# Reordering the state-space stage of a graph network: other PSUM banks for turned slices, products between the logits, interleaved silus

## The reference, cut to what matters

```
fx = x @ W_fx.T + b_fx ; xm = x @ W_x.T + b_x           # 8 heads of 64
sw = softmax((xm @ W_slice.T + b_slice) / temp)         # node -> 64 slices, per head
st = einsum(fx, sw) / (sw.sum(nodes) + 1e-5)            # 64 slice states of 512 per graph
z, xBC, dt = split(st @ in_w.T)                         # the input projection
dt = softplus(dt + dt_bias)                             # both directions
x, B, C = silu(conv3(xBC) + conv_b)
h_t = h_{t-1} * exp(dt A) + dt B x ; y = C h_t          # a scan over the 64 slices, both ways
y = shifted(y_fw) + shifted(y_bw) + x * (x @ fcD_w.T + D)
yg = y * silu(z) ; yg = yg * rsqrt(mean(yg^2)) * norm_w
out = einsum(yg @ out_w.T, sw) @ out_w2.T + out_b       # back from slices to nodes
x = x + out
```

## Time and profile before

| | us |
|---|---|
| time, median of 3 runs | 4348.56 (4342.05 to 4350.47) |
| the profiled execution's own time | 4347.33 |
| its span, first to last instruction | 4345.6 |
| the stage's 13 steady turns, 473.2 to 1671.8 | 1198.6 |
| TensorE busy over the span | 3361.2 (77%) |

### The profile page before, as it was taken

The page is one execution under the profiler, slowest core; times in us unless marked ns, Lnnn a source line. Parts: engine busy times, 40 slices in busy tenths (PEclk is TensorE's granted clock), DMA queues, the critical chain, the costliest instruction groups (busy, mean ns, idle before and its releaser), DMA issues. The chain is left out here.

```text
span 4345.6 us, 58773 instructions
## 1 busy us (share of the span) xinstructions
PE 3361.2 (77%) x22329; PEld 2135.3 (49%) x22329; DVE 2712.3 (62%) x4371; ACT 1291.7 (30%) x2418; POOL 125.4 (3%) x163
## 2 busy tenths in 40 slices
PE   6257999998998998426627997667777797996998
PEld 5134545445454444215514664544444466774665
DVE  4636776777777777499483334488887443884333
ACT  2113333333333333000214443211111341443444
POOL 0000000000000000000000000012222000000000
PEclk6568898999999999655558998688888896887999
DMA  2111111112111112100102331000000210000322
GB/s 34 42 54 40 45 33 45 33 33 52 33 33 45 33 33 49 39 0 0 33 0 70 73 72 13 1 1 0 0 0 4 57 46 10 2 2 21 81 71 66
DMA packets 139573, 141.55 MB, mean 33 GB/s; under 512 B 63764, under 2 KB 121520, under 8 KB 136904
## 3 DMA queue, kind: packets, MB, share of 16 engines
q1 hardware_dynamic: 139376, 138.68, 13.1%
HBM read 130.64 MB, written 8.01 MB: 32 GB/s over the span
## 5 line engine op out<-in xcount | busy, mean ns | idle before, releaser
L733 DVE TENSOR_TENSOR f_hg<-f_hs,f_gb 128x640 f32<-128x640 f32 x320 | 263.8, 825 | 506.5 <-ACT f_hs L715 448.0
L2046 PE MATMUL hy_ps<-hy_uT,hy_win 128*128 128x512 f32 x1152 | 498.7, 593 | 0.0
L715 ACT ACTIVATE f_hs<-f_ph,f_b1t 128x320 f32<-128x320 f32 x640 | 335.0, 527 | 405.0 <-PE f_ph L683 400.9
L683 PE MATMUL f_ph<-XNP,f_w 128*128 (+1 forms) x1280 | 403.3, 439 | 12.8 <-PEq L573 8.6
L698 PE MATMUL f_po<-f_hg,f_w 128*128 128x320 f32 x1280 | 404.4, 439 | 10.5 <-DVE f_hg L733 10.5
L2046 PEld LDWEIGHTS hy_ps<-hy_uT,hy_win 128*128 128x128 f32 x1152 | 217.6, 190 | 281.4 <-issue 281.4
L683 PEld LDWEIGHTS f_ph<-XNP,f_w 128*128 128x128 f32 x1280 | 246.9, 193 | 117.3 <-issue 18.3
L698 PEld LDWEIGHTS f_po<-f_hg,f_w 128*128 128x128 f32 x1280 | 240.1, 191 | 127.3 <-issue 20.9
L1564 PE MATMUL er_g<-er_TP,er_OT 128*128 128x320 bf16 x768 | 148.7, 338 | 125.8 <-ACT er_OT L1533 125.8
L2107 PE MATMUL hy_ps<-hy_wo,hy_yg 128*128 128x512 f32 x512 | 226.8, 602 | 10.8 <-DVE hy_yg L2358 10.8
L1583 PE MATMUL er_c<-XNG 128*128 128x400 f32 x544 | 211.6, 519 | 9.1 <-POOL XNG L1519 9.1
(11 more groups left out here) (489 smaller groups left out, 5988.6 us busy)
## 6 DMA issues: line engine op xcount, KB each, us to landing
f_gb<-gate_rows SPq DMA_DIRECT2D x32, 1280.0 KB, 8.3
XNG<-hy_decays SPq DMA_DIRECT2D x32, 1024.0 KB
hy_rb<-hy_inverse SPq DMA_DIRECT2D x128, 128.0 KB, 3.1
f_gb<-gate_rows SPq DMA_DIRECT2D x16, 640.0 KB, 5.0
hy_xn<-XNP SPq DMA_DIRECT2D x1, 4096.0 KB
hy_XC<-hy_xn SPq DMA_DIRECT2D x16, 256.0 KB, 3.5
XNG<-in_L_ffn_edge_index_dram SPq DMA_DIRECT2D x2, 2048.0 KB
xin<-in_x_dram SPq DMA_DIRECT2D x5, 512.0 KB, 6.7
```

The source lines that it names most:

```text
L683: pe.matmul(psh[e % 2][k][:], w1[:, e, k * 128:(k + 1) * 128], chunk_view(g, c), start=True, stop=True).then_inc(h_ps, 1)
L715: ins = act.activation(hs[:, e % 2, k, :], psh[e % 2][k][:], ACT.Gelu, bias=b1t[:, e * H2 + k:e * H2 + k + 1])
L733: dve.tensor_tensor(hg[:, e % 2], hs[:, e % 2], gb[:, par, e, None, :].broadcast_to([128, H2, CH]), ALU.mult).then_inc(hg_ready, 1)
L2046: mm = pe.matmul(p[:], win[:, t, m * 128:(m + 1) * 128], uT[:, t, :], start=(t == 0), stop=(t == KT - 1))
```

## The change

Four edits, all inside this stage; no computation is added or left out.

- The turned slices 1 and 2 go to banks 4 and 6 in place of 2 and 3. In exchange there are new waits: for `rn` (bank 4 is read by `inverses`) before slice 1, and for a new semaphore `f_out` (bank 6 is read by `out`) before slice 2. The wait for three copies at pair 1's states goes; a wait for one copy stands before slice 3 is turned, and one for two copies before the input projection.
- `logits` is cut in two halves. TensorE's order is now squares, logits of pairs 0 and 1, gains, logits of pairs 2 and 3.
- The silus of the convolved blocks are taken between the silus of z: block 0 after z's 1, blocks 1 and 2 after z's 2, blocks 3 and 4 after z's 3.
- The mean of squares goes to bank 4 in place of 6 and waits for one copy less (`xt_out` 4k + 7 in place of 4k + 8).

```diff
--- before.py
+++ after.py
@@ -1902,12 +1902,13 @@
         oT = uT[:].rearrange("p k n -> p (k n)")[:, 0:KT * CH].rearrange("p (k q j n) -> p k q j n", q=CHP, j=2, n=N)
         s = {n: sem(n) for n in ("xn_st", "xc", "lf_ps", "lg_out", "smx", "sme", "smd", "sn_ps", "rn", "st_ps", "rn_st", "u_out", "sT_ps", "sT_out",
                                  "ip_ps", "ip_out", "cv", "xs", "dtln", "dt_rdy", "da_exp", "da_rdy", "da_ld", "xt_ps", "xt_out",
-                                 "g_ps", "w_rdy", "y_ps", "yg1", "sq", "sq_sum", "r_ps", "rt", "yg2", "ot_ps", "ot_out", "o_ps", "oT_out", "f_ps", "init", "settled")}
+                                 "g_ps", "w_rdy", "y_ps", "yg1", "sq", "sq_sum", "r_ps", "rt", "yg2", "ot_ps", "ot_out", "o_ps", "oT_out", "f_ps", "f_out", "init", "settled")}
         da_st = [sem(f"da_st{i}") for i in range(2)]
         rb_in = [sem(f"rb_in{q}") for q in range(CHP)]
         half = lambda j: slice(SLOT * j, SLOT * (j + 1))
 
-        TURNED = [5, 2, 3, 5]
+        TURNED = [5, 4, 6, 5]
+        CONVOLVED = [[], [0], [1, 2], [3, 4]]
         ORDER = [IPM - 1] + list(range(KT, 2 * KT + 1)) + list(range(KT))
 
         with nc.Block() as spill:
@@ -1987,11 +1988,12 @@
                     pe.wait_ge(sem, value)
                     pe.sem_inc(s["settled"], 1)
 
-            def logits(k):
-
-                pe.wait_ge(s["xc"], 16 * k + 16)
-                wait(pe, s["sT_out"], 4 * k)
-                for q in range(CHP):
+            def logits(k, f):
+
+                if f == 0:
+                    pe.wait_ge(s["xc"], 16 * k + 16)
+                    wait(pe, s["sT_out"], 4 * k)
+                for q in range(2 * f, 2 * f + 2):
                     if q >= 2:
                         pe.wait_ge(s["lg_out"], 4 * k + q - 1)
                     x = XC[:, q * 128:(q + 1) * 128]
@@ -2018,11 +2020,13 @@
                     mm.then_inc(s["sT_ps"], 1)
 
                 for q in range(CHP - 1):
+                    if q == 1:
+                        settle(s["rn"], k + 1)
+                    elif q == 2:
+                        settle(s["f_out"], k + 1)
                     transposed(q)
                 for q in range(CHP):
-                    if q == 1:
-                        settle(s["sT_out"], 4 * k + 3)
-                    elif q >= 2:
+                    if q >= 2:
                         settle(s["u_out"], 4 * k + q - 1)
                     for j in range(2):
                         for h in range(SH_):
@@ -2031,12 +2035,15 @@
                                            sw[rows(j), q, h * 64:(h + 1) * 64], start=True, stop=True)
                     mm.then_inc(s["st_ps"], 1)
                     if q == 1:
+                        settle(s["sT_out"], 4 * k + 1)
                         transposed(CHP - 1)
 
             def input_projection(k):
                 pe.wait_ge(s["u_out"], 4 * k + 4)
                 for i, m in enumerate(ORDER):
-                    if i == 1:
+                    if i == 0:
+                        pe.wait_ge(s["sT_out"], 4 * k + 2)
+                    elif i == 1:
                         pe.wait_ge(s["sT_out"], 4 * k + 4)
                     if i >= 3:
                         pe.wait_ge(s["ip_out"], IPM * k + i - 2)
@@ -2093,8 +2100,8 @@
             def squares(k):
                 pe.wait_ge(s["sq_sum"], k + 1)
                 if there(k + 1):
-                    pe.wait_ge(s["xt_out"], 4 * k + 8)
-                pe.matmul(PS[6][:], g.mean_w[:], sq[:, 0, :], start=True, stop=True).then_inc(s["r_ps"], 1)
+                    pe.wait_ge(s["xt_out"], 4 * k + 7)
+                pe.matmul(PS[4][:], g.mean_w[:], sq[:, 0, :], start=True, stop=True).then_inc(s["r_ps"], 1)
 
             def output_projection(k):
                 pe.wait_ge(s["yg2"], k + 1)
@@ -2137,10 +2144,12 @@
                     steps_down(c + 1)
                 if there(c):
                     squares(c)
+                if there(c + 2):
+                    logits(c + 2, 0)
                 if there(c + 1):
                     gains(c + 1)
                 if there(c + 2):
-                    logits(c + 2)
+                    logits(c + 2, 1)
                 if there(c):
                     output_projection(c)
                     back_to_nodes(c, par)
@@ -2179,6 +2188,8 @@
                     p = PS[4 + i % 3]
                     if m < KT:
                         act.activation(zs[:, par, m, :], p[:], ACT.Silu).then_inc(s["ip_out"], 1)
+                        for b in CONVOLVED[m]:
+                            convolved(k, b)
                     elif m < IPM - 1:
                         if i == 1:
                             wait(act, s["cv"], XB * k)
@@ -2196,13 +2207,13 @@
                         act.wait_ge(s["dt_rdy"], k + 1)
                         act.activation(dA[:], dtv[:], ACT.Exp, scale=negA[:, 0:1]).then_inc(s["da_exp"], 1)
 
-            def convolved(k):
-                for i in range(KT):
-                    act.wait_ge(s["cv"], XB * k + i + 1)
-                    act.activation(xs[:, i, :], xs[:, i, :], ACT.Silu).then_inc(s["xs"], 1)
-                act.wait_ge(s["cv"], XB * k + XB)
-                act.activation(Cs[:], xs[64:128, KT, :], ACT.Silu)
-                act.activation(xs[0:64, KT, :], xs[0:64, KT, :], ACT.Silu).then_inc(s["xs"], 1)
+            def convolved(k, b):
+                act.wait_ge(s["cv"], XB * k + b + 1)
+                if b < KT:
+                    act.activation(xs[:, b, :], xs[:, b, :], ACT.Silu).then_inc(s["xs"], 1)
+                else:
+                    act.activation(Cs[:], xs[64:128, KT, :], ACT.Silu)
+                    act.activation(xs[0:64, KT, :], xs[0:64, KT, :], ACT.Silu).then_inc(s["xs"], 1)
 
             def steps_down(k):
                 for q in range(CHP):
@@ -2220,7 +2231,7 @@
 
             def root(k):
                 act.wait_ge(s["r_ps"], k + 1)
-                act.activation(rr, PS[6][:], ACT.Sqrt, bias=g.eps[:, 0:1], scale=D / DI).then_inc(s["rt"], 1)
+                act.activation(rr, PS[4][:], ACT.Sqrt, bias=g.eps[:, 0:1], scale=D / DI).then_inc(s["rt"], 1)
 
             def out_copy(k, q):
                 act.wait_ge(s["ot_ps"], 4 * k + q + 1)
@@ -2230,7 +2241,6 @@
                 if there(c + 1):
                     slices(c + 1, 1 - par)
                     projected(c + 1, 1 - par)
-                    convolved(c + 1)
                 if there(c):
                     squares(c)
                 if there(c + 1):
@@ -2250,6 +2260,7 @@
             dve.memset(xr[:], 0.0)
             dve.drain()
             dve.nop().then_inc(s["init"], 1)
+            dve.nop().then_inc(s["f_out"], 2)
 
             def softmax(k):
 
@@ -2368,7 +2379,7 @@
             def out(k):
                 dve.wait_ge(s["f_ps"], k + 1)
                 x = chunk_cols(g.XT, k)
-                dve.scalar_tensor_tensor(x, PS[6][:, 0:CH], outb[:, 0:1], x, ALU.add, ALU.add)
+                dve.scalar_tensor_tensor(x, PS[6][:, 0:CH], outb[:, 0:1], x, ALU.add, ALU.add).then_inc(s["f_out"], 1)
 
             def columns(k):
 

```

## The result

| | before | after |
|---|---|---|
| median of 8 runs each, us | 4349.19 (4342.05 to 4353.46) | 4363.92 (4359.22 to 4370.52) |
| ratio, 95% interval | | 1.0036 (1.0025 to 1.0047) |
| the profiled execution | 4347.33 | 4364.72 |
| the stage's 13 steady turns | 1198.6 | 1217.5 |

What follows compares the result with a forecast made beforehand. TensorE and its clock bound the turns: 91.6 clean, -0.5 front, +2.0 at the logits, +0.4 in `steps_down` make 93.5 against 92.2; with end turns 17 us more, 4364. Range 4338 to 4380, the forecast's own 4354 to 4374.

Steps and rivals of the forecast that it cites:

- What sets the end: Stage's turns: nearly all TensorE, so any gain must come from its 8 us idle a turn or its clock.
- Edit 1, a gain of 0.5: Front of the turn: the 2.14 us wait goes, the last load of inverses then limits; 0.5 us a turn gained.
- Edits 3 and 4 in time: `steps_down` starts without its 1.46 us wait, 2.2 idle inside; squares 1.15 earlier, root unmoved; gain 0 from both.
- The wait at the logits: Ahead of the third pair's logits: TensorE idles 3.1 us in place of 1.97, gain 0.
- The clock at the logits: Third pair's logits: clock falls in every turn, 4.0 us at half speed, 2.0 us a turn lost.
- The clock in `steps_down`: Clock falls there in one turn of three, holding root and `yg` by about 1.2 us: 0.4 a turn.
- Two signs that did not come: Signs for after: mean clock of a turn 0.88 to 0.90; 0.50 at the output projection's start in nearly every turn.
- The sum: Per turn: 91.6 - 0.5 + 2.0 + 0.4 = 93.5 against 92.2; 17 us slower in all, 4364.
- it cancels: Rival: clock falls at the logits, only 1.0 us lost, stays in `steps_down`; 92.1 a turn, 4347; chance 0.20.
- The clock stays: Rival: falls as today, front in all turns, middle in six of 13; 91.4 a turn, 4335; chance 0.17.
- each wait goes for good: Rival: the gate and `yg` come earlier too, 4.75 us a turn gained, 66 in all, 4281; chance 0.02.
- both falls in every turn: Rival: clock falls at logits and in `steps_down` every turn (2.3 and 1.2 us); 94.6 a turn, 4380; chance 0.10.

Runs made afterwards that it cites:

- Edit 1: Only turned slices 1 and 2 moved to banks 4 and 6, with their waits, against the kernel before: 4344.86 us, ratio 0.9996.
- edit 3: Only the silus of convolved blocks interleaved with those of z, against the kernel before: 4363.74 us, ratio 1.0044; once more for its profile, 4361.37.
- edit 4: Only the mean of squares moved to bank 4, waiting for one copy less, against the kernel before: 4346.38 us, ratio 1.0003.
- edit 2: Only the logits split in two halves around the gains, against the kernel before: 4361.94 us, ratio 1.0041.
- dense fillers: Changed kernel plus six unread 128x256 products in the wait ahead of the third pair's logits: 4339.75 us, ratio 0.9981 to the kernel before.
- narrow fillers: Changed kernel plus ten unread 128x8 products in the wait ahead of the third pair's logits: 4366.11 us, ratio 1.0039 to the kernel before.

## Why the prediction was right, step by step

**What sets the end.** Right: the sum was to be made of TensorE's clock, not of the three waits. Waits of 4.75 us a turn went, and the turns grew by 1.45.

**Edit 1, a gain of 0.5: the mechanism held.** The dt products start 9.9 us into a turn in the mean of the 13, 10.7 before, with VectorE's last product waiting for its load (above): 0.8 earlier, not 0.5. But they start at half clock, so a part of that is lost again: the restart of the third pair's logits stands 65.61 us into a turn in the mean, 65.95 in the clean turns of before (816.16 - 750.42 = 65.74 in the one of the earlier trace rows), 0.34 earlier.

**Edits 3 and 4 in time.** Right: `steps_down` starts with no wait, 2.26 us are waited ahead of its third pair (2.2 forecast), and where the clock holds the squares come 6.9 us behind VectorE's gate in place of 8.2, so 1.3 sooner (1.15 forecast), while the root stays at 9.5 behind it.

**The wait at the logits.** 3.1 us forecast, 3.37 measured in the turns without a fall in `steps_down`, 2.1 to 2.5 in the others.

**The clock at the logits: right.** In 13 turns of 13. The third and fourth pair's logits take 5.98 us in the mean and took 3.70, so 2.3 in place of 2.0; in the seven turns with no fall before them it is 5.45, 1.75 more. The dense fillers show that this term is the clock's.

**The clock in `steps_down`: its price right by luck, its place wrong, its count too low.** It fell in 6 turns of 13, not in one of three. These six take 94.3 us in the mean and the other seven 93.1, the 1.2 of the forecast. But the price was said to come through the root and `yg`, held up by 1.2. Measured, the logits' restart is only 0.2 later in the six (65.72 us into the turn against 65.52). Counted from VectorE's gate, which comes 0.3 earlier in the six, root, `yg` and restart are held up by 0.46, where the forecast had 1.2. The other 1.0 comes behind the restart: when the clock has fallen in `steps_down` it comes back and falls again later, and that second fall covers nearly all of the restarted logits, 6.6 us against 5.45. The timeline of a turn without the fall, to set beside the 2.08 us from 817.52 above:

```profile
724.06 2.07 PE L2000 MATMUL hy_ps<-hy_wlg,hy_XC 128*128 128x512 f32 x2 [3.37 <-DVE hy_fx L2270]
725.93 1.72 PE L2001 MATMUL hy_ps<-hy_wfx,hy_XC 128*128 128x512 f32 x2
727.48 1.02 PE L2000 MATMUL hy_ps<-hy_wlg,hy_XC 128*128 128x512 f32 x2
```

The clock is back within the second group. The same groups of the turn from 751.7, the first of which stands above:

```profile
819.39 1.91 PE L2001 MATMUL hy_ps<-hy_wfx,hy_XC 128*128 128x512 f32 x2
821.10 1.91 PE L2000 MATMUL hy_ps<-hy_wlg,hy_XC 128*128 128x512 f32 x2
822.80 1.07 PE L2001 MATMUL hy_ps<-hy_wfx,hy_XC 128*128 128x512 f32 x2
```

Here the third is still at half clock.

**Two signs that did not come.** I had named a mean clock of a turn of 0.88 to 0.90, and 0.50 at the start of the output projection. The turns read 0.91 to 0.94, and the clock is back ahead of the output projection in all 13. The second did not follow from my own numbers: with 4.0 us at half clock the logits themselves take 5.7 us, so it is over before they end. Measured, the clock is at half for 3.55 us behind the restart in the seven turns and 5.9 in the six. The mean clock is higher because the half clock in the front became shorter, 6.8 us in ten of 13 turns in place of 10.2 in all of them; its end still lies on the dt products, which take 5.7 us (5.6 before), so that this gave nothing.

**The sum.** Cut at the logits' restart, a clean turn of before is 65.95 + 25.64 = 91.6; a turn of after is 65.61 + 28.04 = 93.65. So -0.34 ahead of the restart (forecast: -0.5 and +0.4) and +2.40 behind it (forecast +2.0; 2.3 of it is the logits themselves, which hold the 1.0 of the six turns as well). Each forecast term is off by up to 0.4, and that the time came out at 4364 to the microsecond is luck. Part of it is the first turn, 4 us shorter, which no step had. The single edits place it: that turn takes 82.0 us with the silus alone and 85.5 with the split logits alone, 88.7 and 89.2 with edits 1 and 4. It has no gate, squares or output behind which a gain could be lost; what exactly it gains there stays open. Two of my side sums are off: *it cancels* gives 14 x -0.1 - 1, so -2.4 us in all and 4345, not 4347; and with both terms of the range at their far ends the sum gives 4346 to 4379, not 4354 to 4374. Neither changes a reading.

**Single edits do not add up.** Edits 1 and 4 alone do nothing, edit 2 costs 16 us, edit 3 costs 18 (14 in its one further run), and all four together cost 15. Each fall shifts or replaces the next one: with the silus alone, the fall in `steps_down` runs through squares and logits; with the split as well, there is one at the logits whatever the silus do. I had not forecast this. Taken for each edit alone, the terms of my sum are wrong for edit 1 (-0.5 a turn; measured 0) and edit 3 (+0.4; measured 1219.1 - 1198.6 = 20.5 in 13 turns, 1.6).

**The rivals.** *The clock stays* falls with the windows at the logits; *it cancels* with the 3.2 us or more, in every turn, for which the clock is at half behind their restart; *each wait goes for good* with the waits that took their place; *both falls in every turn* with 7 turns of 13 that have one.

The Trainium skill, "TensorE: Matmul & The Clock Gate", section "A second HAM failure mode: psum-queue depth-cycling", puts such losses down to what is paid for the clock's fall and return between bursts; the runs with dense and narrow fillers agree, 4339.75 against 4366.11.

## What to carry to other kernels

Two short waits merged into one longer can cost more than the two did, if TensorE's clock falls behind them: price a wait by the speed of the work that follows it, and look at the granted clock there before and after an edit. Test it with dense products that nothing reads, put into the wait; if the time drops, and does not drop with narrow products in their place, the clock was the cause. The fillers may be kept, as long as they end before the wait does at half speed too. Don't add up edits measured singly where the falls of the clock can shift.

## What the runs showed of the hardware

- Ten products of 128x8 in the wait left the logits behind it at half clock in 13 turns of 13; behind six of 128x256 they ran at full clock in 13 of 13, though in eleven of these the clock still fell and came back while the fillers ran.
- Half clock cost nothing where a wait followed it (edit 4, a fall in every turn, ratio 1.0003), and 2 us a turn where it lay on the work behind the last wait (edit 2, ratio 1.0041).
- The falls form a pattern over turns: clean and slow turns alternate in before, but for three clean ones in a row; with the silus alone, turns of 94.4 to 94.9 and of 92.7 to 93.3 us alternate. With a small gain in one place (0.7 in the front, edit 1) all turns were of one kind.
- Holding the clock in most of one stage made the changed kernel 0.75% faster than the one before (ratio 0.9925), though extra work was added: TensorE's busy time in the 13 turns rose from 1098.28 in the kernel after to 1143.16, while they got 42 us shorter.
